# Mamba-2 block with adaLN on one core: decay exponents from broadcast rows of sums and a per-partition column, in place of a TensorE product

## What is computed

```python
A_log = xBCzA[..., 3072:]                      # 64 heads, 16 wide; 8 groups share B and C
dt = softplus(A_log);  dA = -dt
A_cum = cumsum(dA within a chunk)
L[i, j] = exp(A_cum[i] - A_cum[j]) if j <= i else 0
Y_diag = einsum('bcshn,bczhn,bhcsz,bczhp->bcshp', C, B, L, X)   # X = x
states = B^T . exp(A_cum[-1] - A_cum) . X;  Y_off = C . carried state . exp(A_cum)
y = (Y_diag + Y_off + D x / dt) * silu(z + z_bias);  out = y @ out_proj_w.T
```

## Time and profile before

| | |
|---|---|
| median of 3 runs | 658.55 us (657.72 to 658.92) |
| the profiled execution's own time | 658.04 us |
| its span, first to last instruction | 656.3 us |
| TensorE / weight loads busy | 93% / 73% |
| VectorE, ScalarE, GpSimd busy | 77%, 58%, 54% |
| mean granted TensorE clock | 0.990 |
| DMA | 70.5 MB, mean 107 GB/s |

### The profile page before, as it was taken

The page is one execution under the profiler, slowest core; times in us unless marked ns, Lnnn a source line. Parts: engine busy times, 40 slices in busy tenths (PEclk is TensorE's granted clock), DMA queues, the critical chain, the costliest instruction groups (busy, mean ns, idle before and its releaser), DMA issues.

```text
span 656.3 us, 21241 instructions
## 1 busy us (share of the span) xinstructions
PE 612.0 (93%) x8345; PEld 481.2 (73%) x8345; DVE 504.1 (77%) x928; ACT 383.8 (58%) x844; POOL 355.8 (54%) x411
## 2 busy tenths in 40 slices
PE   2788899999999999999999999999997999999995
PEld 1565677787787777878777787787875777888884
DVE  6797799978778787787977778778695566787756
ACT  2788555456465455655545655656664437566565
POOL 4776114347537355554543755547574657766642
PEclk9799999999999999999999999999999999999999
DMA  8734120613221221421222253231325735444411
GB/s 296 224 131 163 39 67 29 203 66 103 67 92 60 83 72 54 148 74 41 70 76 100 88 152 102 70 120 64 97 71 166 224 106 147 137 129 128 129 49 64
DMA packets 59866, 70.52 MB, mean 107 GB/s; under 512 B 13972, under 2 KB 33460, under 8 KB 59256
## 3 DMA queue, kind: packets, MB, share of 16 engines
q1 hardware_dynamic: 59768, 69.17, 33.0%
HBM read 54.45 MB, written 14.70 MB: 105 GB/s over the span
## 4 chain that ended last, share of the span: by engine, by line
PE 78%; DVE 7%; POOL 4%; issue 4%; ACT 3%; DMA 3%; SPq 1%; POOLq 0%; DVEq 0%; ACTq 0%
PE bank L1218 37%; PE bank L1985 12%; PE pair L1283 7%; PE bank L1227 4%; PE bank L2018 4%; PE pair L1256 3%; PE bank L1313 2%; PE bank L1236 2%; PE pair L1269 2%; DVE m_cv L1472 1%; POOL h_lo L435 1%; PE pair L1296 1%; DMA h_lo_place<-y_scratch 1%; PE bank L1245 1%; DVE p_xn L514 1%
## 5 line engine op out<-in xcount | busy, mean ns | idle before, releaser
L1472 DVE SCALAR_TENSOR_TENSOR m_cv<-bank,gpc,m_cv 128x511 f32<-128x511 f32 (+2 forms) x192 | 143.5, 748 | 36.0 <-ACT m_cv L1375 31.5
L1218 PE MATMUL bank<-h_hi,w_hi 128*128 128x512 f32 x384 | 163.2, 425 | 1.6 <-POOL h_lo L435 1.5
L1218 PE MATMUL bank<-h_hi,w_lo 128*128 128x512 f32 x384 | 152.0, 396 | 0.0
L1218 PE MATMUL bank<-h_lo,w_hi 128*128 128x512 f32 x384 | 151.4, 394 | 0.0
L1387 ACT ACTIVATE m_M<-bank 128x512 f32<-128x512 f32 x128 | 76.1, 594 | 65.9 <-PE bank L1227 64.1
L1375 ACT ACTIVATE m_cv<-bank,gpc 128x512 f32<-128x512 f32 x96 | 72.0, 750 | 72.6 <-PE bank L1218 72.1
L1614 POOL TENSOR_TENSOR m_S<-m_S,m_cd 128x128 f32<-128x128 f32 x96 | 40.2, 419 | 126.5 <-DVE m_S L1535 65.4
L1218 PEld LDWEIGHTS bank<-h_hi,w_hi 128*128 128x128 f32 x384 | 73.1, 190 | 22.1 <-issue 3.1
L1604 POOL TENSOR_TENSOR m_Xw<-m_Xp,wend 128x256 f32<-128x256 f32 x64 | 39.8, 622 | 85.4 <-ACT m_Xp L1395 85.4
L1218 PEld LDWEIGHTS bank<-h_hi,w_lo 128*128 128x128 f32 x384 | 72.5, 189 | 16.7
L1502 DVE TENSOR_TENSOR m_M<-m_M,pair 128x512 f32<-128x512 f32 x128 | 81.8, 680 | 0.3 <-issue 0.3
(11 more groups left out here) (179 smaller groups left out, 1228.9 us busy)
## 6 DMA issues: line engine op xcount, KB each, us to landing
m_ea<-ea_scratch SPq DMA_DIRECT2D x32, 256.0 KB
m_dd<-dd_scratch SPq DMA_DIRECT2D x32, 256.0 KB
y_scratch<-m_t SPq DMA_DIRECT2D x16, 512.0 KB, 3.4
h_lo_place<-y_scratch SPq DMA_DIRECT2D x16, 512.0 KB, 4.5
p_wm<-in_L_wmod_dram SPq DMA_DIRECT2D x6, 1024.0 KB, 6.7
m_wraw<-in_L_attn_in_proj_w_dram SPq DMA_DIRECT2D x18, 256.0 KB, 3.4
w_lo_place<-in_L_attn_input__dram SPq DMA_DIRECT2D x16, 256.0 KB, 4.8
out_dram<-t_o SPq DMA_DIRECT2D x16, 256.0 KB, 2.3
```

The lines of the kernel that those rows point to most:

```text
L1218: ins = pe.matmul(A[k % 3][:, :], w[:, t, kc, :], h[:, n % NB, kc, :], start=(m == 0), stop=(m == 11))
L1472: ins = dve.scalar_tensor_tensor(out=cv[:, k % 3, lag:], in0=A[k % 3][:, 0:L - lag], scalar=s.gpc[:, gp, o:o + 1], in1=cv[:, k % 3, lag:], ...
```

## The change

- The 128 matmuls `decay(u, q)`, the tiles `R` and `Lm`, their constants and the high/low split of the sums go.
- The sums are stored once per half of the batches as rows, one per pair of groups, batch and chunk (`store_sums`, 8 DMAs). `load_decays(u)` broadcasts two such rows of 4 KB to 64 partitions each, so a tile `sums` (`T`, two buffers) of 128x1024 holds A_cum[s] of 16 heads: 512 KB for a unit.
- The own sums, A_cum[z] negated, come into columns `less` once per half of the batches, by four transposes (`less_turn`) and four copies.
- Group q = 0: `exponent_of_heads` makes 8 ScalarE instructions of 128x64, exp with the head's column as bias. Group q = 1: GpSimd adds the columns to `sums` (`less_sums`, 128x512) one iteration ahead, and `exponent` takes exp of it from SBUF. `spread` stands ahead of the exponents in slot 2.
- The triangle is applied to the Gram matrix instead, in PSUM (`mask`, one VectorE instruction of 128x128 for a unit), and `mix` becomes min(m, 1) times the Gram matrix, since exp is unbounded above the diagonal.
- In the first part two `less_sums` stand ahead of the last four `low_part` on GpSimd. SyncE's loads of sums wait for `exp_done` instead of `d_done`.

```diff
+    def store_sums(sp, pb):
+        sp.wait_ge(a_v[pb], A_SUM)
+        for n in range(2 * GP):
+            rows = slice(2 * HG * n, 2 * HG * n + 2 * HG)
+            sp.dma_start(s.a_d[2 * GP * pb + n].rearrange("c (m s) -> m c s", s=Q),
+                         s.chain[rows, pb, 3, :].rearrange("m (c s) -> m c s", s=Q)).then_inc(d_scr[pb], 16)
+        sp.wait_ge(d_scr[pb], 2 * GP * 16)
...
-        for n in range(8, 16):
+        for n in range(8, 12):
             low_part(n)
+        less_sums(pool, 0)
+        less_sums(pool, 1)
+        for n in range(12, 16):
+            low_part(n)
+        chunk_starts(1)
         pool.wait_ge(t_pe, 16)
         pool.memset(s.Xp[:, :, :, :], 0.0).then_inc(zeroed, 1)
...
                 for c in range(2):
-                    first = R_POS + 2 * c
-                    sp.dma_start(s.R[first:first + 2, u % 2, :, :].bitcast(F32).rearrange("r q (h s) -> r (q h) s", s=Q),
-                                 a_v[:, b, gp, :, chunk(u, c)]).then_inc(rl_ready[u % 2], 16)
-                for r in range(2):
-                    first = R_NEG + HG * r
-                    sp.dma_start(s.Lm[first:first + HG, u % 2, :, :].bitcast(F32),
-                                 na_v[r, b, gp, :, :, tok(u)]).then_inc(rl_ready[u % 2], 16)
+                    row = a_v[b, gp, 2 * (u % UPS) + c:2 * (u % UPS) + c + 1, :]
+                    sp.dma_start(s.T[Q * c:Q * c + Q, u % 2, :, :].rearrange("p q n -> p (q n)"),
+                                 row.broadcast_to([Q, 2 * HG * Q])).then_inc(rl_ready[u % 2], 16)
...
-                    sp.wait_ge(d_done, 2 * (v + 2) + 2)
+                    sp.wait_ge(exp_done, 2 * (v + 2) + 2)
                     load_decays(v + 4)
...
-            def decay(u, q):
-
-                if q == 0:
-                    pe.wait_ge(rl_ready[u % 2], 64 * (u // 2 + 1))
-                wait(pe, exp_done, 2 * u + q)
-                pe.matmul(DB[:, :], s.Lm[:, u % 2, q, :], s.R[:, u % 2, q, :], start=True, stop=True).then_inc(d_done, 1)
...
-            def exponent(u, q):
-                act.wait_ge(d_done, 2 * u + q + 1)
+            def exponent_of_heads(u):
+
+                gp, b, i = u // (NB * UPS), u // UPS % NB, u % UPS
+                act.wait_ge(rl_ready[u % 2], 32 * (u // 2 + 1))
+                act.wait_ge(start.le_ev, UPS if b < 2 and gp == 0 else 2 * UPS)
                 wait(act, yd_done, u - 1)
-                act.activation(M[:, u % 2, q, :], DB[:, :], ACT.Exp).then_inc(exp_done, 1)
+                for h in range(HG):
+                    cols = slice(h * Q, h * Q + Q)
+                    ins = act.activation(M[:, u % 2, 0, cols], s.T[:, u % 2, 0, cols], ACT.Exp, bias=s.less[:, gp, b, i, h:h + 1])
+                ins.then_inc(exp_done, 1)
+
+            def exponent(u):
+                act.wait_ge(taken, u + 1)
+                wait(act, yd_done, u - 1)
+                act.activation(M[:, u % 2, 1, :], s.T[:, u % 2, 1, :], ACT.Exp).then_inc(exp_done, 1)
...
                     if sl == 2 and u < NU:
-                        exponent(u, 0)
                         spread(u)
+                        exponent_of_heads(u)
...
+            def mask(u):
+                dve.wait_ge(g_done, u + 1)
+                g = YS[:, :, 384:384 + Q]
+                dve.tensor_tensor(g, g, s.tri[:, :].unsqueeze(1).broadcast_to([P, 2, Q]), ALU.mult).then_inc(mask_done, 1)
...
-                dve.tensor_tensor(m, m, g, ALU.mult).then_inc(m_done, 1)
+                dve.scalar_tensor_tensor(out=m, in0=m, scalar=1.0, in1=g, op0=ALU.min, op1=ALU.mult).then_inc(m_done, 1)
...
+            def less_sums(pool, u):
+                gp, b, i = u // (NB * UPS), u // UPS % NB, u % UPS
+                pool.wait_ge(rl_ready[u % 2], 32 * (u // 2 + 1))
+                pool.wait_ge(start.le_ev, UPS if b < 2 and gp == 0 else 2 * UPS)
+                sums = s.T[:, u % 2, 1, :].rearrange("p (h s) -> p h s", s=Q)
+                pool.tensor_tensor(sums, sums, s.less[:, gp, b, i, HG:2 * HG].unsqueeze(2).broadcast_to([P, HG, Q]),
+                                   ALU.add).then_inc(taken, 1)
...
                 if v > 0 and i == (2 if n == 0 else 1):
                     skip(n, 0)
                     skip(n, 1)
+                if 2 <= v + 3 < NU:
+                    less_sums(pool, v + 3)
```

More of the change, by code:

```diff
@@ L557, in vector @@
         sums(dve, 0)
-        normalize(12)
-        low_sums(dve, 0)
-        for i in range(13, 16):
+        for i in range(12, 16):
             normalize(i)
+        less_copy_first(dve)
         convolve(0)
@@ L623, in sums, with less_of, less_copy_first, less_copy_second @@
                           ALU.subtract).then_inc(a_v[pb], 1)
-    def low_sums(dve, pb):
-        hi, pl = s.chain[:, pb, 2, :], s.chain[:, pb, 3, :]
-        dve.wait_ge(a_act[pb], B_CD)
-        dve.tensor_tensor(pl, pl, hi, ALU.subtract).then_inc(a_v[pb], 1)
+    def less_of(pb, i):
+        return (s.less[:, :, 2 * pb:2 * pb + 2, i, :],
+                s.DB[:, i * P:(i + 1) * P].rearrange("p (q g h) -> p g q h", q=2, g=GP))
+    def less_copy_first(dve):
+        dve.wait_ge(le_pe, 1)
+        for i in range(UPS):
+            dst, src = less_of(0, i)
+            dve.tensor_scalar(dst, src, -1.0, None, ALU.mult).then_inc(le_ev, 1)
+    def less_copy_second(act):
+        act.wait_ge(le_pe, 2)
+        for i in range(UPS):
+            dst, src = less_of(1, i)
+            act.activation(dst, src, ACT.Copy, scale=-1.0).then_inc(le_ev, 1)
     def skips(dve, pb):
@@ L638, in decays @@
     def decays(act, pb):
-        end, hi, pl, ea = (s.chain[:, pb, i, :] for i in (1, 2, 3, 4))
+        end, pl, ea = (s.chain[:, pb, i, :] for i in (1, 3, 4))
         act.wait_ge(a_v[pb], A_END)
-        act.activation(hi.bitcast(F32R), pl, ACT.Copy).then_inc(a_act[pb], 1)
         act.activation(ea, pl, ACT.Exp).then_inc(a_act[pb], 1)
@@ L764, in end_turn, with less_turn @@
         ins.then_inc(we_pe, 1)
+    def less_turn(pe, pb):
+        pe.wait_ge(a_v[pb], A_SUM)
+        if pb == 0:
+            pe.wait_ge(h_act, 9)
+        for i in range(UPS):
+            ins = pe.transpose(s.DB[:, i * P:(i + 1) * P], s.chain[:, pb, 3, i * P:(i + 1) * P], s.ident[:, :])
+        ins.then_inc(le_pe, 1)
     def turn_rows(pe, late):
@@ L1157, in sync @@
                 if v == 3:
+                    start.store_sums(sp, 1)
                     start.store_decays(sp, 1)
```

140 lines of the change are left out of this document (57 added, 83 removed).

## The result

The changed kernel takes 693.75 us (median of 4 runs, 684.35 to 699.47), the kernel before 658.13 in the same comparison: ratio 1.0467, 95% interval 1.042 to 1.0515. By the lowest of each (684.35 against 657.03) it is slower by 27 us, by the medians by 36, where 646 with a range to 667 was forecast. The profiled execution took 695.72 us, its span is 694.0. Where two changed kernels are compared, the difference of the medians stands first, and beside it, where it says something else, that of the ratios times 657 us. Where the intervals of two ratios overlap, their difference is not clear of the scatter.

A forecast was written before the change was run, and what follows sets the result against it. TensorE was taken to set the pace in the loop's middle. From 658.04 us, -25.4 for the decays, +1.5 for the first part and other stretches and +12 for the short exponents' place gave 646 us, range 631 to 667.

The forecast's parts named there:

- What a decay costs TensorE: Decay matmuls on TensorE: each priced start to start at 0.235 us, 0.47 us a unit, not 443 ns busy.
- 54 x 0.47: TensorE's gain over the loop, leaving out 10 of 64 units: 25.4 us.
- What the others get: Added loads a unit: ScalarE +1.45 us net, VectorE +0.22, GpSimd +1.29; no engine over the new unit of 6.50 us.
- Where they stand: First slots of a step: short exponents delay linear part, taps and mix; 0.85 us a step given back, 12 us.
- upper bound of this step of the prediction: Two narrow places a step instead of one: 1.7 us a step given back, 24 us in all.
- elsewhere the exponents were waiting for TensorE anyway: ScalarE outside the first slots: 64.1 us of waits over the loop pay for most of the additions.
- DMA ... I cost them at nothing except as a rival: Loads of sums, 32 to 512 KB a unit, 32 MB more, issued an iteration ahead: no cost.
- recorded sign: Sign that the forecast is wrong: GpSimd waiting 3 us a step for a DMA, and TensorE in turn for it.
- the sums come late at GpSimd: Rival: at a step's start sums queue behind store and scales, 35 us lost, 669 us; chance 0.24.
- First part and other stretches: Before and around the loop's middle: constants gone, additions ahead of low parts, VectorE's units; +1.5 us in sum.
- 0 to 5 us lost: First part: two additions on GpSimd ahead of four low parts and the clearing of Xp; taken as 2.5 us.
- 1.7 to 1.9 us a step given back: Rival that it cancels: short exponents at 0.33 us or a second narrow place, 656.5 to 659.5 us; chance 0.08.

The follow-up runs named there:

- e5: Changed kernel with thinned sums, one 128x512 exponent in place of eight short ones, and skips of step 1 loaded ahead of the stores: 643.61 us.
- e3: Changed kernel with GpSimd's addition of the own sum cut from 128x512 to 128x16 elements: 693.65 us.
- e1: Changed kernel with each load of sums from unit 2 on writing 2 partitions instead of 64, instructions and waits kept: 672.06 us.
- e11: Changed kernel with thinned sums, skips of step 1 ahead of the stores, and the eight short exponents one slot earlier: 651.61 us.
- e9: As e8, but the eight short exponents at the end of slot 1, ahead of the linear part: 661.15 us.
- e6: Changed kernel with the load of the skips of step 1 moved ahead of the second half's stores of sums: 695.65 us.
- e13: As e9, with early exponents behind the copy of x, unit 3's store wait one unit later, most last-part loads behind the last sums: 657.13 us.
- e15: Changed kernel with the short exponents at the end of slot 1 and none of SP's order changes: 689.97 us.
- e8: Changed kernel with scales loaded one unit later, skips of step 1 ahead of the stores, short exponents ahead of the copy of x: 682.1 us.

## Why the prediction was wrong

Two steps failed. The bytes of the sums, put at nothing, cost 17 to 22 us, and the place of the short exponents, put at 12 us, cost some 24 to 28 together with the exponents. A third, the count of units in which TensorE gains, was 6 us too hopeful.

**"What a decay costs TensorE": right in price, too high in count.** 0.44 us a unit (e5) where 0.47 stood; 443 ns of busy time was indeed the wrong number. The Trainium skill, Perfetto Trace Analysis, section Identifying the Most-Contended Engine, judges TensorE by the busy share of the weight loads, beside its share of peak arithmetic. By that share, 79% in the middle, a unit would have gained some 0.37 us (an estimate); the trace bears out the starts. But "54 x 0.47" counted nearly every unit of the loop's middle, because TensorE was 99% busy there. In the first unit of each step the chain goes over linear part, taps and xs (e5), and nothing comes back: 12.8 us over 36 units are 0.36 a unit, so 54 units give 19, not 25.4. A busy engine isn't the bound of every unit: there the chain over ScalarE and VectorE had no slack, which following it through each of the four units could have told.

**"What the others get": right.** Eight short exponents take 2.01 us, 0.25 each, for 1.9 forecast; the second exponent 0.62; min-and-multiply 683 ns. The addition on GpSimd takes 1046 ns, not 1292, and is free (e3). Nothing slows VectorE: its taps take 747 ns, 748 before. The Trainium skill, SBUF — State Buffer, section Who interferes with whom, has just this for VectorE instructions with at most one SBUF input. `mask` wasn't tried alone.

**"Where they stand": the step that failed first.** The forecast saw one narrow place a step, the first slot 2, and took 0.85 us for it, 12 us in all. The middle gave back all of the 15.5 us between 250.6 (e1) and 235.1 (e5), 1.7 us a step, with one exponent for eight: the upper bound of this step of the prediction (two places, 1.7 a step, 24 us) was the true value. Over the whole kernel e1 lies 28.5 us over e5, up to 4.5 of them the order of the skips (e11). The second place is the chain of e1 above, copy of x, exponents, mix. The argument "elsewhere the exponents were waiting for TensorE anyway" spent that wait on work that stands behind it: the exponents came after the linear part and the copy, which still wait for TensorE. Filling a wait takes an instruction ahead of it in the queue, as in e9.

**"DMA ... I cost them at nothing except as a rival": the step that failed most.** Full bytes cost 21.7 us by the medians (changed kernel against e1), 17 by the ratios. The recorded sign of it came: GpSimd waited 65.9 us for sums, 4 a step. The rival "the sums come late at GpSimd" named the queue, the bytes and the place, and had 0.24 at 669 us; its 35 us for late landings were more than the 22 found. What it had wrong is what the rate decides: at a step's start DMA moves some 230 GB/s, close to the 240 of the earlier trace rows, and the sums are late even so. The landing shown is 10.0 us after its issue. Up to it 1.5 MB were issued, 0.75 MB more behind it within 4 us, and some 2.4 MB had moved from 452 to 466, so it came with the last of all that and not after its own 1.5 MB. And the issue itself was late, since SP stands behind the output store's wait. ScalarE waits as well, which the rival hadn't.

**"First part and other stretches": wrong in size.** The first `diagonal` came 1.5 us earlier, where 1.0 later was forecast, but units 0-7 took 18.5 us more, for 0.5 forecast. The largest piece is at unit 7, SP's queue again (chain, start, us):

```profile
124.56 1.80 DMA a_scratch<-chain
...
126.38 0.34 SPq L373
...
127.27 3.73 DMA cd_scratch<-p_cde
...
136.92 0.61 SPq L1103
137.57 10.95 DMA m_dd<-dd_scratch
...
153.10 0.70 PE pair L1268 x8
```

Eight scratch stores for two (5 us of issuing), two waits for stores in the middle of the order where one stood before, then sums, store and scales ahead of the skips. The forecast went through ScalarE, VectorE and GpSimd for this stretch and left out SP, whose work had grown most there. With the skips moved ahead (e6) a late landing of sums took the place. The gate rows behind waiting exponents (4.4 us on VectorE in e9) and the first addition ahead of `low_part` (e13) are of the same kind. The latter the forecast saw ("0 to 5 us lost").

**The sum that the runs give**, from the kernel before's 656, a chain of differences that closes by construction: removal with additions, mask and one exponent, -12 (e5); eight exponents for one, +8 (e11); their place, +20 (e1; up to 4.5 of it the skips); bytes that land late, +22; 694. By the ratios the last term is 17, and the end 688. Each step is a difference of two runs, and the second and third aren't independent of the fourth: e15 shows that a slot earlier gains nothing clear while the sums are late, and e9 21 us with the queue in better order. One slip of the recorded sums changes nothing: 1.7 to 1.9 us a step given back is 658 to 661 us, not 656.5 to 659.5. What is left open is how much of the 8 us of e11 could be covered as well, what `mask` costs alone, and which part of the loss from unit 44 on in the changed kernel belongs to the last part's weights in the same queue.

## What to carry to other kernels

Operands moved from an engine's matmul to a broadcast DMA turn 32 KB into 512 KB; what decided here was not the mean rate (149 GB/s in the middle) but what stood in the same in-order queue at a step's start, so write out that queue with its waits and bytes before costing it at nothing. Work added to a queue fills a wait only if it stands ahead of the instruction that waits: the same eight instructions, put there, took 21 us less (e8 to e9), and nothing clear while their own input came late (e15). And a mean of 99% busy doesn't make each unit that engine's: look at the periods one by one.
